# Five hand-laid instruction lists of a pipelined attention and FFN layer are laid in a new order

## The reference, cut to what matters

```
Q, K, V = split into 16 heads of 8 (x @ Wq.T + bq, x @ Wk.T + bk, x @ Wv.T + bv)
scores  = Q K^T / sqrt(8);  masked where key > query;  minus (query - key)
att     = softmax(scores) V;  y = layernorm(x + att @ Wo.T + bo)
h = silu(y @ w1.T * s1) * (y @ w2.T * s2)          # 128 -> 512
h = gelu(h @ h1.T * g1);  h = gelu(h @ h2.T * g2)  # 512 -> 512, exact gelu
out = layernorm(y + h @ w3.T * s3)                 # 512 -> 128
```

## Time and profile before

| | us |
|---|---|
| median of 3 runs | 764.61 (764.49 to 766.36) |
| span of the profiled execution | 763.0 |
| PE busy | 721.0 (94%) |
| DVE busy | 590.4 (77%) |
| ACT busy | 551.7 (72%) |
| POOL busy | 509.7 (67%) |

### The profile page before, as it was taken

The page is one execution under the profiler, slowest core; times in us unless marked ns, Lnnn a source line. Parts: engine busy times, 40 slices in busy tenths (PEclk is TensorE's granted clock), DMA queues, the critical chain, the costliest instruction groups (busy, mean ns, idle before and its releaser), DMA issues.

```text
span 763.0 us, 18187 instructions
## 1 busy us (share of the span) xinstructions
PE 721.0 (94%) x5993; PEld 496.8 (65%) x5993; DVE 590.4 (77%) x2761; ACT 551.7 (72%) x876; POOL 509.7 (67%) x616
## 2 busy tenths in 40 slices
PE   4798999999999999999999999999999999999995
...
GB/s 238 170 35 32 111 46 9 133 30 121 45 108 55 45 105 17 128 37 114 51 75 78 17 133 30 120 46 111 52 64 86 17 131 21 119 33 24 25 1 29
DMA packets 56367, 54.18 MB, mean 71 GB/s; under 512 B 28048, under 2 KB 36496, under 8 KB 56272
## 3 DMA queue, kind: packets, MB, share of 16 engines
...
...
## 4 chain that ended last, share of the span: by engine, by line
PE 57%; ACT 13%; DVE 12%; issue 8%; SPq 4%; DMA 3%; POOL 2%; POOLq 0%; DVEq 0%; ACTq 0%
PE ps L586 18%; PE ps L592 15%; DVE ps L964 7%; ACT pt L809 5%; PE ps L631 5%; PE ps L690 5%; PE ps L671 3%; PE ps L605 3%; ACT sg L859 3%; PE ps L699 2%; DVE m L964 2%; ACT L809 2%; PE ps L612 1%; DMA sums<-raw 1%; ACT k_hi L800 1%
## 5 line engine op out<-in xcount | busy, mean ns | idle before, releaser
L964 DVE CUSTOM_DVE_ANT_0 ps<-ps,causal 128x256 f32<-128x256 f32 (+1 forms) x928 | 297.4, 392 | 21.6 <-PE ps L634 21.4
L1108 POOL TENSOR_SCALAR_AFFINE_SELECT pt<-pt 128x512 f32<-128x512 f32 x256 | 160.6, 637 | 97.7 <-ACT pt L809 92.5
L1151 POOL TENSOR_TENSOR hlo<-hf,hhi 128x512 fp32r<-128x512 f32 x128 | 163.9, 1286 | 91.9 <-ACT hhi L894 90.4
L809 ACT ACTIVATE pt<-ps 128x768 f32<-128x768 f32 x256 | 194.7, 811 | 26.8 <-PE ps L673 24.4
L884 ACT ACTIVATE hf<-ps,vec_sb 128x512 f32<-128x512 f32 x128 | 86.2, 684 | 99.7 <-PE ps L592 99.7
L586 PE MATMUL ps<-hhi,h_hi 128*128 128x512 f32 x496 | 146.0, 415 | 0.3 <-ACT hhi L894 0.3
L592 PE MATMUL ps<-hlo,h_hi 128*128 128x512 f32 x496 | 139.5, 398 | 1.2 <-POOL hlo L1157 0.7
L964 DVE DVE_READ_ACCUMULATOR2_ANT m<- 128x1 f32 x928 | 130.4, 141 | 0.0
L592 PEld LDWEIGHTS ps<-hlo,h_hi 128*128 128x128 f32 x496 | 93.3, 188 | 28.8 <-POOL hlo L1157 6.3
L690 PE MATMUL ps<-pt,vst 128*32 128x256 f32 (+1 forms) x2048 | 106.5, 337 | 0.1
L586 PEld LDWEIGHTS ps<-hhi,h_hi 128*128 128x128 f32 x496 | 85.3, 188 | 20.5 <-ACT hhi L894 0.7
...
## 6 DMA issues: line engine op xcount, KB each, us to landing
...
den<-sums SPq DMA_DIRECT2D x128, 32.0 KB, 1.9
...
```

The lines of the kernel that those rows point to most:

```text
L809: nc.scalar.activation(pt[u][:, c:c + 2, :], ps[:, first:last + 1, 0:3 * P], ACT.Exp).then_inc(t_free.sem, 1)
L964: part = nc.vector.tensor_tensor_reduce(ps[:, bank, cols], ps[:, bank, cols], mask, 1.0, LOWEST, ALU.add, ALU.max, m32[b][:, max_col(c + e ...
L1108: nc.gpsimd.affine_select(out=diag, in_=diag, compare_op=ALU.is_ge, fill=0.0, base=0, pattern=[[0, 2], [0, 2], [1, P]], channel_multiplier ...
L1151: nc.gpsimd.tensor_tensor(h_lo[layer % 2][:, m, :], hf[:, n % 4, :], h_hi[layer % 2][:, m, :].bitcast(F32), ALU.subtract).then_inc(hlo_rea ...
```

## The change

The lists `PE_ORDER`, `ACT_ORDER`, `DVE_ORDER`, `POOL_ORDER` and `SP_ORDER` hold the same steps in another order. Fill, drain and every step's instructions and waits stay. What moves:
- PE: `s` 0,0 and 0,1 are set apart by a `pv`; `mT` 0 goes behind `s` 1,1 and 1,2; `x1t` ahead of `s` 1,4; `qq` and `w3h` ahead of `g` 0; `s` 1,7 behind them, next to `st` 0,0; `qk` and `u` 0 follow; `w3l` is followed by `mT` 1; `zt` stands ahead of `g` 2; `pv` 0,2 and 0,3 and `pv` 1,0 and 1,1 become neighbours; the slot ends on `st` 1,6 and 1,7.
- ACT: `ghi` 0 and 1 and the `tanh` are placed anew between the `exp`; `table` moves.
- DVE: `arec` 0 is first; `x1lo` goes ahead of `smax` 1,5, `qlo` 0 ahead of `smax` 1,7; `gmul` 0 and 1 later, `vadd` ahead of `gmul` 2.
- POOL: `hlo` 1,0 goes ahead of `amul` 0 and `xbo`, `amul` 1 ahead of `hlo` 1,1; `rstd` 2 ahead of `sel` 0,6; `glo` 0 and 1 are placed anew.
- SP: `repack` and `spread` of sequence 0 are mixed with the `gather` of sequence 1; `qstack` goes ahead of `mTd` 1; `xload` and `tload` move to the end.

```
 PE_ORDER = [
-    ("u", 3, -2), ("s", 0, 0, 0), ("s", 0, 1, 0), ("pv", 1, 2, -1), ("pv", 1, 3, -1), ("s", 0, 2, 0), ("h", 1, 0, -2),
...
-    ("s", 1, 6, 0), ("s", 1, 7, 0), ("qq", 1), ("g", 0, -1), ("u", 0, -1), ("w3h", -2), ("st", 0, 0, 0),
-    ("st", 0, 1, 0), ("qk", 1), ("w3l", -2), ("st", 0, 2, 0), ("st", 0, 3, 0), ("u", 1, -1), ("g", 1, -1),
...
-    ("pv", 1, 0, 0), ("st", 1, 6, 0), ("st", 1, 7, 0), ("pv", 1, 1, 0),
+    ("u", 3, -2), ("s", 0, 0, 0), ("pv", 1, 2, -1), ("s", 0, 1, 0), ("pv", 1, 3, -1), ("s", 0, 2, 0),
+    ("h", 1, 0, -2), ("s", 0, 3, 0), ("s", 0, 4, 0), ("h", 1, 1, -2), ("h", 1, 2, -2), ("s", 0, 5, 0),
+    ("s", 0, 6, 0), ("h", 1, 3, -2), ("s", 0, 7, 0), ("wo", -1), ("s", 1, 0, 0), ("h", 2, 0, -2), ("s", 1, 1, 0),
+    ("s", 1, 2, 0), ("mT", 0, 0), ("h", 2, 1, -2), ("s", 1, 3, 0), ("h", 2, 2, -2), ("x1t", -1), ("s", 1, 4, 0),
+    ("s", 1, 5, 0), ("h", 2, 3, -2), ("s", 1, 6, 0), ("qq", 1), ("w3h", -2), ("g", 0, -1), ("s", 1, 7, 0),
+    ("st", 0, 0, 0), ("qk", 1), ("u", 0, -1), ("st", 0, 1, 0), ("st", 0, 2, 0), ("w3l", -2), ("mT", 1, 0),
+    ("g", 1, -1), ("st", 0, 3, 0), ("st", 0, 4, 0), ("pv", 0, 0, 0), ("zt", 2, -2), ("st", 0, 5, 0), ("g", 2, -1),
+    ("u", 1, -1), ("st", 0, 6, 0), ("st", 0, 7, 0), ("pv", 0, 1, 0), ("u", 2, -1), ("st", 1, 0, 0), ("st", 1, 1, 0),
+    ("pv", 0, 2, 0), ("pv", 0, 3, 0), ("st", 1, 2, 0), ("st", 1, 3, 0), ("g", 3, -1), ("qv", 1), ("st", 1, 4, 0),
+    ("st", 1, 5, 0), ("pv", 1, 0, 0), ("pv", 1, 1, 0), ("st", 1, 6, 0), ("st", 1, 7, 0),
 ]
 ACT_ORDER = [
...
+    ("gelu", 2, 3, -2), ("hhi", 2, 3, -2), ("qhi", 0, 1), ("tanh", 0, -1), ("exp", 0, 0, 0), ("qhi", 1, 1),
+    ("exp", 0, 1, 0), ("exp", 0, 2, 0), ("tanh", 1, -1), ("exp", 0, 3, 0), ("exp", 0, 4, 0), ("exp", 0, 5, 0),
+    ("tanh", 2, -1), ("exp", 0, 6, 0), ("exp", 0, 7, 0), ("ghi", 0, -1), ("exp", 1, 0, 0), ("exp", 1, 1, 0),
+    ("ghi", 1, -1), ("exp", 1, 2, 0), ("exp", 1, 3, 0), ("tanh", 3, -1), ("exp", 1, 4, 0), ("exp", 1, 5, 0),
+    ("exp", 1, 6, 0), ("exp", 1, 7, 0), ("table", "exp", 0), ("ghi", 2, -1), ("ghi", 3, -1), ("araw", 1, 0),
...
 POOL_ORDER = [
-    ("glo", 2, -2), ("glo", 3, -2), ("xbo", -1), ("amul", 0, -1), ("hlo", 1, 0, -2), ("hlo", 1, 1, -2),
-    ("amul", 1, -1), ("hlo", 1, 2, -2), ("hlo", 1, 3, -2), ("rstd", 1, -1), ("hlo", 2, 0, -2), ("hlo", 2, 1, -2),
+    ("glo", 2, -2), ("glo", 3, -2), ("hlo", 1, 0, -2), ("amul", 0, -1), ("xbo", -1), ("amul", 1, -1),
+    ("hlo", 1, 1, -2), ("hlo", 1, 2, -2), ("hlo", 1, 3, -2), ("rstd", 1, -1), ("hlo", 2, 0, -2), ("hlo", 2, 1, -2),
...
 SP_ORDER = [
...
+    ("gather", 0, 0, -1), ("repack", 0, 0, -1), ("gather", 0, 1, -1), ("repack", 0, 1, -1), ("spread", 0, 0, -1),
+    ("spread", 0, 1, -1), ("gather", 1, 0, -1), ("gather", 1, 1, -1), ("repack", 1, 0, -1), ("spread", 0, 2, -1),
+    ("spread", 0, 3, -1), ("spread", 1, 0, -1), ("repack", 1, 1, -1), ("spread", 1, 1, -1), ("spread", 1, 2, -1),
+    ("spread", 1, 3, -1), ("mTd", 0, 0, 0), ("mTd", 0, 1, 0), ("qstack", 1), ("mTd", 1, 0, 0), ("mTd", 1, 1, 0),
+    ("kstack", 1), ("xload", 2), ("store", -2), ("tload", 0),
 ]
```

More of the change, by code:

```diff
@@ L147 @@
     ("gelu", 1, 3, -2), ("hhi", 1, 3, -2), ("gelu", 2, 0, -2), ("hhi", 2, 0, -2), ("lnnorm", 1, -1),
[L148 to L155, removed]
+    ("gelu", 2, 1, -2), ("gelu", 2, 2, -2), ("x1hi", -1), ("x1c", -1), ("hhi", 2, 1, -2), ("hhi", 2, 2, -2),
+    ("gelu", 2, 3, -2), ("hhi", 2, 3, -2), ("qhi", 0, 1), ("tanh", 0, -1), ("exp", 0, 0, 0), ("qhi", 1, 1),
@@ new lines @@
+    ("exp", 0, 1, 0), ("exp", 0, 2, 0), ("tanh", 1, -1), ("exp", 0, 3, 0), ("exp", 0, 4, 0), ("exp", 0, 5, 0),
+    ("tanh", 2, -1), ("exp", 0, 6, 0), ("exp", 0, 7, 0), ("ghi", 0, -1), ("exp", 1, 0, 0), ("exp", 1, 1, 0),
+    ("ghi", 1, -1), ("exp", 1, 2, 0), ("exp", 1, 3, 0), ("tanh", 3, -1), ("exp", 1, 4, 0), ("exp", 1, 5, 0),
+    ("exp", 1, 6, 0), ("exp", 1, 7, 0), ("table", "exp", 0), ("ghi", 2, -1), ("ghi", 3, -1), ("araw", 1, 0),
+    ("gelu", 1, 0, -1), ("hhi", 1, 0, -1), ("gelu", 1, 1, -1), ("table", "gelu", 0), ("hhi", 1, 1, -1),
@@ L156 @@
+    ("gelu", 1, 2, -1), ("hhi", 1, 2, -1),
 ]
 DVE_ORDER = [
-    ("gate", 3, -2), ("arec", 0, -1), ("gmul", 3, -2), ("smax", 0, 0, 0), ("smax", 0, 1, 0), ("smax", 0, 2, 0),
+    ("arec", 0, -1), ("gate", 3, -2), ("gmul", 3, -2), ("smax", 0, 0, 0), ("smax", 0, 1, 0), ("smax", 0, 2, 0),
     ("arec", 1, -1), ("smax", 0, 3, 0), ("smax", 0, 4, 0), ("smax", 0, 5, 0), ("smax", 0, 6, 0), ("smax", 0, 7, 0),
-    ("res1", -1), ("smax", 1, 0, 0), ("lnstat", 1, -1), ("smax", 1, 1, 0), ("smax", 1, 2, 0), ("mTc", 0, 0),
@@ L161 @@
[L161 to L164, removed]
+    ("res1", -1), ("smax", 1, 0, 0), ("lnstat", 1, -1), ("smax", 1, 1, 0), ("mTc", 0, 0), ("smax", 1, 2, 0),
+    ("mTl", 0, 0), ("smax", 1, 3, 0), ("smax", 1, 4, 0), ("x1lo", -1), ("smax", 1, 5, 0), ("smax", 1, 6, 0),
@@ L165 @@
+    ("qlo", 0, 1), ("smax", 1, 7, 0), ("gate", 0, -1), ("qlo", 1, 1), ("res2", -2), ("mTc", 1, 0), ("mTl", 1, 0),
+    ("gate", 1, -1), ("gmul", 0, -1), ("lnstat", 2, -2), ("gmul", 1, -1), ("gate", 2, -1), ("lnnorm", 2, -2),
+    ("araw", 0, 0), ("vadd", 1), ("gmul", 2, -1),
 ]
 POOL_ORDER = [
-    ("glo", 2, -2), ("glo", 3, -2), ("xbo", -1), ("amul", 0, -1), ("hlo", 1, 0, -2), ("hlo", 1, 1, -2),
-    ("amul", 1, -1), ("hlo", 1, 2, -2), ("hlo", 1, 3, -2), ("rstd", 1, -1), ("hlo", 2, 0, -2), ("hlo", 2, 1, -2),
+    ("glo", 2, -2), ("glo", 3, -2), ("hlo", 1, 0, -2), ("amul", 0, -1), ("xbo", -1), ("amul", 1, -1),
@@ L169 @@
+    ("hlo", 1, 1, -2), ("hlo", 1, 2, -2), ("hlo", 1, 3, -2), ("rstd", 1, -1), ("hlo", 2, 0, -2), ("hlo", 2, 1, -2),
     ("hlo", 2, 2, -2), ("hlo", 2, 3, -2), ("sel", 0, 0, 0), ("sel", 0, 1, 0), ("sel", 0, 2, 0), ("sel", 0, 3, 0),
-    ("sel", 0, 4, 0), ("sel", 0, 5, 0), ("sel", 0, 6, 0), ("sel", 0, 7, 0), ("rstd", 2, -2), ("sel", 1, 0, 0),
-    ("glo", 0, -1), ("sel", 1, 1, 0), ("sel", 1, 2, 0), ("sel", 1, 3, 0), ("sel", 1, 4, 0), ("sel", 1, 5, 0),
-    ("sel", 1, 6, 0), ("sel", 1, 7, 0), ("glo", 1, -1),
+    ("sel", 0, 4, 0), ("sel", 0, 5, 0), ("rstd", 2, -2), ("sel", 0, 6, 0), ("sel", 0, 7, 0), ("glo", 0, -1),
@@ L173 @@
+    ("sel", 1, 0, 0), ("sel", 1, 1, 0), ("sel", 1, 2, 0), ("sel", 1, 3, 0), ("glo", 1, -1), ("sel", 1, 4, 0),
+    ("sel", 1, 5, 0), ("sel", 1, 6, 0), ("sel", 1, 7, 0),
 ]
 SP_ORDER = [
-    ("gather", 0, 0, -1), ("gather", 0, 1, -1), ("repack", 0, 0, -1), ("repack", 0, 1, -1), ("spread", 0, 0, -1),
-    ("spread", 0, 1, -1), ("spread", 0, 2, -1), ("spread", 0, 3, -1), ("gather", 1, 0, -1), ("gather", 1, 1, -1),
-    ("repack", 1, 0, -1), ("repack", 1, 1, -1), ("spread", 1, 0, -1), ("spread", 1, 1, -1), ("spread", 1, 2, -1),
@@ L178 @@
-    ("spread", 1, 3, -1), ("xload", 2), ("tload", 0), ("mTd", 0, 0, 0), ("mTd", 0, 1, 0), ("mTd", 1, 0, 0),
-    ("mTd", 1, 1, 0), ("kstack", 1), ("qstack", 1), ("store", -2),
+    ("gather", 0, 0, -1), ("repack", 0, 0, -1), ("gather", 0, 1, -1), ("repack", 0, 1, -1), ("spread", 0, 0, -1),
+    ("spread", 0, 1, -1), ("gather", 1, 0, -1), ("gather", 1, 1, -1), ("repack", 1, 0, -1), ("spread", 0, 2, -1),
+    ("spread", 0, 3, -1), ("spread", 1, 0, -1), ("repack", 1, 1, -1), ("spread", 1, 1, -1), ("spread", 1, 2, -1),
```

## The result

| | before | after |
|---|---|---|
| median of 4 runs, us | 765.24 (764.49 to 766.36) | 778.71 (776.35 to 782.45) |
| span of the profiled execution, us | 763.0 | 774.5 |
| ratio of the times | 1 | 1.018 (1.0157 to 1.0203) |

The new order is 1.8% slower, 13.5 us by the medians and 11.5 us by the two profiled executions. The forecast was 770 with a range of 760 to 776. The kernel did get slower, but by more than twice what was forecast, and 778.71 lies outside the range.

A forecast was written before the change was run, and what follows sets the result against it. PE, busy in 94% of the span, was taken as the bound. 24.7 up to `qq` plus 19.2 after gave 43.9 per slot against 43.43: +0.48, times 13 is +6.2 us, so 770 us, range 760 to 776.

The forecast's parts named there:

- The two added waits: `st` 0,2 waits 1.06 us for the first `exp`; `h` 2,0 waits 0.3 for `hlo` 1,3, held back by `amul` 1.
- The waits at `s` 0,2, `h` 1,0, `s` 1,7 and `qq`: PE's waits before `qq`, 0.31, 0.28, 0.34 and 0.18 us, 1.11 together, were to go.
- back part: The slot from `qq` on: 18.40 us before, forecast 19.2 with 1.52 of added waits.
- Front part: The slot up to `qq`: 24.94 us before, forecast 24.7 including the `hlo` wait.
- `exp` 1,6 ... +0.10: At the next slot's start, `exp` 1,6 ends at 0.75 where `s` 0,0 asks at 0.67: 0.10 us more.
- `hlo` behind `amul` 1 ... I take 0.3: On POOL `amul` 1 delays three `hlo`, so `h` 2,0 waits 0.3 us, bounds 0 and 0.8.
- 2.2, if `rstd` 2 ... makes `pv` 0,3 wait as well: Upper bound of the waits added after `qq`, 2.2 us, if `rstd` 2 ahead of `sel` 0,6 delays `pv` 0,3.
- the two passages at 0.20: After `qq`, two more switches between 32-row and 128-row matmuls on PE, about 0.10 us each, +0.20.
- I give the seams nothing, 0.5 either way: Outside the 13 counted slots, with fill and drain lists kept, no change was forecast, 0.5 us either way.
- That the `hlo` wait doesn't appear: At `h` 2,0, `spread` transfers land in time: slot 43.6, +2.3 us, 767; chance 0.2.
- The faster case: From `st` 0,2 on, ACT keeps ahead of PE: slot 43.0, -5.6 us, 759; chance 0.22.
- The last rival: Attention's chain is later and `wo` also waits for `amul` 1: slot 44.5, +14 us, 778; chance 0.1.

The follow-up runs named there:

- the first two edits together: The changed kernel with `amul` 1 behind `hlo` 1,1 on POOL and `g` 0 directly behind `qq` on PE: 760.45 us, ratio 0.9952 to the kernel before.
- run 14: Not a follow-up run: in "The lists run 14 slots" the word is a verb, and the lists go through 14 slots.

## Why the prediction was right in kind and short in size

**Right.** The two added waits stand where the prediction put them, for the reasons it gave. `st` 0,2 waits 1.06, the forecast value, behind the same table load. The Trainium skill's 1.38 of drain behind each load (ScalarE: Activation LUTs, What ACT_TABLE_LOAD costs) is not in this trace: `exp` starts 0.01 behind the load in the rows of after as in those with `tanh` 0 moved. `amul` 1 starts at 11.77 (forecast 11.7) and the last `hlo` ends at 16.22 (16.2). The waits at `s` 0,2, `h` 1,0, `s` 1,7 and `qq` went. In the back part `st` 1,1 waits 0.20 and `st` 1,7 0.15 (forecast 0.20 and 0.19). Front part 24.90 against 24.7, back part 19.34 against 19.2.

**The terms of the sum that were too small.** The forecast was +0.48 a slot, the profiled slots show 9.84 / 13 = +0.76. The waits of a slot were forecast at 1.92 together (0.10, 0.3 and 1.52) and measure about 2.4:
- "`exp` 1,6 ... +0.10" at `s` 0,0. The `exp` ends 0.76 into the slot, as forecast, but `s` 0,0 starts at 0.91 and not at 0.77. I had put nothing between the end of a releasing instruction and PE's start. That is 0.14 more.
- "`hlo` behind `amul` 1 ... I take 0.3". The wait is 0.42: 0.35 by the rows, and the release on top. Rounding down was the wrong way. 0.12 more.
- `pv` 0,0 waits 0.14, which I had not seen. It needs `res2` (L1072), which needs `w3l`, and `w3l` stands behind `st` 0,2. The wait is there with `g` 0 early too, where `st` 0,2 still waits, and gone in both kernels that have `tanh` 0 behind `exp` 0,0, where it doesn't. So it looks like a part of the same chain, which my sum closed at `st` 0,2.
- `pv` 0,3 waits 0.12 for `sel` 0,7, with `rstd` 2 ahead of `sel` 0,6. I had named this one as a bound ("2.2, if `rstd` 2 ... makes `pv` 0,3 wait as well") and given it nothing in the sum. No run moves `rstd` 2 back.
- `st` 1,3, where I had put 0.07, doesn't wait; `st` 1,5 does, 0.10.

These make about 0.5. Against them PE's own work was counted about 0.2 too high: without its waits the front part takes 24.24 and not 24.31, and the back part about 17.57 and not 17.69, so the two passages at 0.20 were too dear. What is left is 0.32: a slot of 44.24 where the sum had 43.92. Over 13 slots, 44.26 on average, that is 4.4 us. The base gives 1.0 of it back: I had taken 43.43 from one `st` 0,0 to the next, which takes in the start of the shorter last slot, and from `u` 3 to `u` 3 the kernel before has 43.51. To rounding, that is the 3.6 below.

**"I give the seams nothing, 0.5 either way".** This failed by 2.2 us in the last slot. The lists run 14 slots and my sum counts 13, so the 0.9 that a full slot lost (44.24 against 43.34) was missing once already. The other 1.3 is of the last slot alone. Without `qq`, `qk` and `qv` PE has about 2.1 us less to do there; before, the slot got 1.3 shorter by it. Now it doesn't: 44.27 against 44.24. PE in the last slot of the changed kernel:

```profile
685.40 1.13 PE L699 MATMUL ps<-wo_sb,attT 128*128 128x128 f32 x8 [0.23 <-POOL attT L1132]
...
699.92 0.39 PE L671 MATMUL ps<-qs,ks 32*128 32x256 f32 x2
...
701.59 0.39 PE L671 MATMUL ps<-qs,ks 32*128 32x256 f32 x2 [0.57 <-DVE m L964]
...
702.65 0.39 PE L671 MATMUL ps<-qs,ks 32*128 32x256 f32 x2 [0.61 <-ACT pt L809]
```

`wo` waits for `amul` 1 and starts 0.30 later than in a full slot, and `h` 2,0 takes 0.14 more. `qk` isn't there to cover `smax` 1,7, and `st` 0,1 waits 0.57 for it; `st` 0,2 waits for ACT as in every slot. With `amul` 1 moved the last slot is 43.70, with `g` 0 early 43.29, with both 42.69: 1.58 of the 2.2 hang on the two placements. The rest I have not taken apart.

**Sum.** Of the 5.3 us between the forecast +6.2 and the +11.5 of the profiled executions, 3.6 are the slots, 2.2 the last slot, and the ends give back 0.5. The other 2 us of the 13.5 lie between the profiled execution and the median: the profiled execution of the changed kernel was its fastest, at a mean granted clock of 0.957; the other three took 778.56, 782.45 and 778.86 at 0.955, 0.952 and 0.955. More stretches at half clock in those runs would account for it. In the kernel of the first two edits together such a stretch did go with a slow execution: the profiled one, 763.26 at 0.954, has 6.8 us at half clock in its first full slot and loses 2.7 us there, and five of the others took 759.9 to 760.5. For the changed kernel's own runs there are no traces, and it stays argued.

**The rivals.** That the `hlo` wait doesn't appear fell with the first trace. The faster case decided at an added wait under 0.5 at `st` 0,2; the wait is 1.06, and with it cured, by either edit, the kernel is level or 0.2% faster, and with `hlo` cured too 0.5% faster. Its estimate of 759 is close to the 760.45 measured with both waits gone, so the gain existed, and the two placements cost over three times as much. The last rival, that `wo` waits for `amul` 1 as well, comes true in three of 14 slots: by 0.13 in slots 4 and 5, which are the longer ones, and by 0.30 in the last. Its 778 is next to the measured 778.71 by chance: it wanted 0.4 in every slot, and most of the loss it would explain came from elsewhere. My own 770 was a little low by its own sum, too: 764.61 + 6.2 is 770.8.
